# Three probability tiles of a Perceiver kernel turned by DMA instead of TensorE, and weight loads moved behind the experts

## The reference, cut to what matters

```python
# first cross attention (16 heads of 64), keys beyond a length masked out
scores = einsum('bhmk,bhnk->bhmn', Q, K);  scores = where(mask == 0, -1e20, scores)
attn = softmax(scores / 8);  ctx = einsum('bhmn,bhnv->bhmv', attn, V);  x = x + ctx @ W_o
# small self attention on the 64 tokens, then a mixture of 8 experts
x = x + self_attention(layernorm(x)) ; x = x + experts(layernorm(x))
# second cross attention over the same context, then the delta-rule mixer (weights d_w, w1s)
# last feed-forward part: weights quantised to 8 bit, which needs the largest |w| of each channel
amax = clip(max(abs(w)), 1e-8);  scale = 127 / amax;  w_q = clip(round(w * scale), -128, 127) / scale
```

## Time and profile before

| | us |
|---|---|
| median of 3 runs | 409.58 |
| lowest, highest | 409.54, 411.42 |
| profiled execution, its own time | 409.08 |
| its span | 407.3 |
| TensorE busy | 382.6 (94%) |
| TensorE weight loads, beside it | 296.9 (73%) |
| VectorE busy | 287.2 (71%) |
| ScalarE busy | 287.6 (71%) |
| GpSimd busy | 237.9 (58%) |

### The profile page before, as it was taken

One profiled execution on the slowest core, in us unless ns is written; L12 is line 12 of the kernel. 1 busy time (PEld: TensorE's weight loads), 2 busy tenths in 40 slices (PEclk: granted clock), 3 DMA queues, 4 the chain that ended last, 5 costly groups with the idle time before them and its releaser, 6 DMA issues.

```text
span 407.3 us, 11598 instructions
## 1 busy us (share of the span) xinstructions
PE 382.6 (94%) x4632; PEld 296.9 (73%) x4632; DVE 287.2 (71%) x730; ACT 287.6 (71%) x568; POOL 237.9 (58%) x196
## 2 busy tenths in 40 slices
PE   6988999999998999988989999999999999999995
PEld 3446777777776778967966777777777769878874
DVE  2788888888875777566767767877787777454544
ACT  3477888888787887746429988899888987544240
POOL 2497989999974659301006997877788668030000
PEclk9899999999999999998999999999999999999999
DMA  8899998989999998990005999999999999600000
GB/s 305 323 253 167 201 182 134 178 147 212 228 184 210 223 178 132 338 408 21 3 2 84 185 200 207 195 196 191 194 193 191 189 199 188 276 2 3 2 2 3
DMA packets 188390, 68.56 MB, mean 168 GB/s; under 512 B 183200, under 2 KB 183984, under 8 KB 187440
## 3 DMA queue, kind: packets, MB, share of 16 engines
q1 hardware_dynamic: 188048, 66.77, 82.2%
q10 hardware_dynamic: 288, 1.05, 0.8%
HBM read 21.90 MB, written 0.03 MB: 54 GB/s over the span
## 4 chain that ended last, share of the span: by engine, by line
PE 46%; DVE 17%; DMA 10%; POOL 10%; ACT 9%; issue 7%; SPq 0%; POOLq 0%; DVEq 0%; ACTq 0%
PE ps L521 17%; PE ps L489 13%; DMA probsT<-halves 9%; DVE probs L640 8%; POOL halves L593 7%; ACT probs L558 3%; PE ps L501 2%; ACT halves L565 2%; PE ps L1097 2%; DMA moe<-in_ctxT 2%; PE ps L764 1%; DVE U L653 1%; PE ps L1204 1%; DVE halves L593 1%; PE ps L774 1%
## 5 line engine op out<-in xcount | busy, mean ns | idle before, releaser
L593 POOL TENSOR_TENSOR halves<-probs,halves 128x896 f16<-128x896 f32 x75 | 141.7, 1892 | 55.2 <-ACT halves L565 53.7
L521 PE MATMUL ps<-ctxN,probsT 128*128 128x128 f16 x2352 | 148.4, 219 | 4.2 <-DMA probsT<-halves 4.1
L521 PEld LDWEIGHTS ps<-ctxN,probsT 128*128 128x128 f16 x2352 | 139.4, 98 | 17.8 <-issue 7.0
L489 PE MATMUL ps<-ctxT_parts,GT_parts 128*128 128x512 f16 (+1 forms) x660 | 143.0, 353 | 5.6 <-DVE negmax L640 5.4
L558 ACT ACTIVATE probs<-probs,shifted 128x896 f32<-128x896 f32 x112 | 115.5, 1031 | 6.7 <-DVE shifted L645 6.7
L489 PEld LDWEIGHTS ps<-ctxT_parts,GT_parts 128*128 128x128 f16 x660 | 59.6, 98 | 54.9 <-DVE negmax L640 7.6
L565 ACT CAST halves<-probs 128x896 f16<-128x896 f32 x93 | 85.8, 923 | 0.0
L653 DVE SCALAR_TENSOR_TENSOR U<-U,alpha,ps 128x128 f32<-128x128 f32 x112 | 38.6, 345 | 55.2 <-PE ps L521 54.9
L640 DVE CUSTOM_DVE_ANT_0 probs<-ps,zero,negmax 128x896 f32<-128x896 f32 x56 | 67.5, 1205 | 1.7 <-POOL halves L593 1.2
L640 DVE CUSTOM_DVE_ANT_0 probs<-ps,maskb,negmax 128x896 f32<-128x896 f32 x56 | 67.5, 1205 | 1.6 <-issue 0.7
L555 ACT ACTIVATE alpha<-negmax 128x1 f32<-128x1 f32 x96 | 28.2, 294 | 37.8 <-DVE negmax L640 36.6
(11 more groups left out here) (368 smaller groups left out, 388.7 us busy)
## 6 DMA issues: line engine op xcount, KB each, us to landing
moe<-in_ctxT SPq DMA_DIRECT2D x7, 448.0 KB, 7.6
moe<-in_mask SPq DMA_DIRECT2D x6, 448.0 KB, 10.1
moe<-in_gateT SPq DMA_DIRECT2D x2, 1024.0 KB, 9.3
moe<-in_upT SPq DMA_DIRECT2D x2, 1024.0 KB, 11.0
moe<-in_downT SPq DMA_DIRECT2D x2, 1024.0 KB, 13.7
moe<-in_fir_long SPq DMA_DIRECT2D x1, 2048.0 KB, 9.7
probsT<-halves SPq DMA_TRANSPOSE x93, 4.8
wv<-in_wv SPq DMA_DIRECT2D x2, 512.0 KB, 7.1
```

What stands on the lines that cost most here:

```text
L489: ins = pe.matmul(ps[:, 2 * b + h, 0:width], GT_parts[:, g_part, r * P:(r + 1) * P], ctxT_parts[:, keys:keys + width], start=(g_part == 0 ...
L521: ins = pe.matmul(ps[:, bank, 0:D], probsT_parts[:, b, p_part, k * P:(k + 1) * P], ctxN_parts[:, at:at + D], start=(p_part == 0 and c_part ...
L593: eng.tensor_tensor(halves_of(L, n)[:, 1, :], probs[:, n % BUFS, :], halves_of(L, n)[:, 0, :], ALU.subtract).then_inc(lower_of(L, n)[0], 1)
```

## The change

Tiles 15, 31 and 47 of the first attention are no longer turned on TensorE: they go by DMA, and VectorE does their halving. `win`, `wout`, `d_w` and `w1s` are no longer loaded between the transpositions of the first attention but behind the expert loads, ahead of the wait for `y_ready`; `a_w` moves from tile 40 to tile 36. The channel maxima of `win` and `wout` move on VectorE from before `y_ready` to behind the probabilities of the small self attention.

```diff
         WEIGHTS_AT = {24: ("in1", w_qT, "wqT1"), 27: ("in1", wkT[:], "wkT1"), 30: ("out0", wv[:], "wv0"),
-                      33: ("out0", wo[:], "wo0"), 36: ("ffn", win[:], "win"), 38: ("ffn", wout[:], "wout"),
-                      40: ("small_attn", a_w[:], "a_w"), 42: ("delta", d_w[:], "d_w"), 44: ("delta", w1s[:], "w1s")}
+                      33: ("out0", wo[:], "wo0"), 36: ("small_attn", a_w[:], "a_w")}
 
         def on_pe(L, n):
-            return L == 0 and n % 4 == 3 and n > 4 or n >= STEPS - 3 or n == STEPS - 5
+            return L == 0 and n % 4 == 3 and n % 16 != 15 and n > 4 or n >= STEPS - 3 or n == STEPS - 5
 
         def on_vector(L, n):
             if L == 0:
-                return n in (0, 2) or 4 <= n < 30 and n % 4 == 1
+                return n in (0, 2) or 4 <= n < 30 and n % 4 == 1 or n % 16 == 15
             return n >= RAMP and n % 4 == 3
@@ SP's queue
             load_experts(0)
             load_experts(1)
+            load("ffn", win[:], "win")
+            load("ffn", wout[:], "wout")
+            load("delta", d_w[:], "d_w")
+            load("delta", w1s[:], "w1s")
             sp.wait_ge(sem("y_ready"), 1)
@@ VectorE, behind project_dve(dve, 0)
-            loaded(dve, "ffn")
-            for i, w in enumerate((win, wout)):
-                ins = dve.tensor_reduce(wamx[:, i * FT:(i + 1) * FT], w[:], AX, ALU.max, apply_absolute_value=True)
-            seq(ins)
             loaded(dve, "par")
@@ VectorE, behind the second half of a_probs
+            loaded(dve, "ffn")
+            for i, w in enumerate((win, wout)):
+                ins = dve.tensor_reduce(wamx[:, i * FT:(i + 1) * FT], w[:], AX, ALU.max, apply_absolute_value=True)
+            seq(ins)
             seq(dve.tensor_scalar(wamx[:], wamx[:], 1e-8, None, ALU.max))
```

## The result

The changed kernel took 410.74 us (median of 20 runs, 408.81 to 413.52) beside 409.56 us for the kernel before on the same chip (median of 20 runs); the ratio is 1.0031, 95% interval [1.0016, 1.0046]. That is inside the predicted range and inside the 0.5% that were called no change, but it is a small loss and not nothing. The sum of the forecast came close; several of its parts did not.

A forecast was written before the change was run, and what follows sets the result against it. The prediction took the loop as tight in several places, TensorE having 46% of the chain of waits. Its terms, 0 + 0 - 0.4 + 0 + 0.65 = +0.25 us, gave 409.6 us, range 407.6 to 411.6.

The forecast's parts named there:

- Tile 15, 0: First attention: GpSimd's gapless work holds the maximum of tile 20 at 70.77, so no gain; bounds -0.76 and +0.5 us.
- Rival 3: Tile 15: GpSimd's mask conversion blocks VectorE's new halving, about +1 us, 410.6; chance 0.06.
- Tile 31, 0: First attention: halving waits up to 0.9 us for GpSimd, later given back; 0, bounds -0.76 and plus one transposition, 2.4 us.
- that is given back in front of GpSimd's halving of tile 33: Tile 31: the halving's delay of up to 0.9 us vanishes where tile 37's maximum waits for GpSimd anyway.
- rival 2: Tile 31: the DMA queue takes over, one transposition of 2.4 us added to tile 34's landing, total +2.65, 412.0; chance 0.11.
- Tile 47, -0.4: End of first attention: VectorE's halving fits a gap before tile 43's addition; gain 0.4 us, bounds -0.76 and 0.
- it carries to the end: Tile 47: the 0.4 us gain passes through GpSimd's chain and the last transposition to the end of the first attention.
- Loads, 0: Moving weight loads out of the first attention gains 0, since TensorE waits for no landing from 125 to 161 us.
- Maxima, +0.65: Behind the small self attention's probabilities: the two reductions, 1.28 us, make the copy of `oT` 0.65 us late, nothing absorbing it.
- Rival 4: The maxima run under cover because the `oT` copy is late for another reason: -0.4 us, 409.1; chance 0.11.
- Rival 1: TensorE bounds the whole first attention and all three turns come off: -1.65 us, 407.8; chance 0.18.
- Rival 5: `win` and `wout` land late and VectorE waits, each microsecond over 3 us of delay counting in full; chance 0.02.

The follow-up runs named there:

- e7: The kernel before with tile 31 alone turned by DMA and halved by VectorE; ratio to before 1.0009 [0.9987, 1.0031].
- e1: The kernel before with tiles 15, 31 and 47 by DMA, loads and maxima at their old places; ratio to before 1.0045 [1.0018, 1.0071].
- e4: The changed kernel with `wo` loaded after tile 38 instead of 33; ratio to before 0.9997 [0.9974, 1.0020].
- e6: The changed kernel with the warm-up between the attentions replaced by one of about 44 more TensorE instructions; ratio to before 1.0054 [1.0032, 1.0077].
- e8: The kernel before with tile 47 alone turned by DMA and halved by VectorE; ratio to before 1.0012 [0.9992, 1.0031].
- e2: The changed kernel with tiles turned as before, so only loads and maxima are moved; ratio to before 1.0003 [0.9981, 1.0025].
- e5: The kernel before with 44 fewer TensorE warm-up instructions between the attentions, 12 instead of 56; ratio to before 1.0015 [0.9996, 1.0035].
- e9: The kernel before with tile 15 alone turned by DMA and halved by VectorE; ratio to before 1.0006 [0.9986, 1.0026].
- e12: The changed kernel with turns as before, `wo` behind tile 38, maxima in VectorE's gaps among the experts; ratio to before 0.9970 [0.9947, 0.9994].
- e10: The kernel before with the load of `wo` moved from behind tile 33 to behind tile 39; ratio to before 0.9994 [0.9977, 1.0010].
- e11: The kernel before with `wo` loaded behind tile 32 instead of 33 and `win` behind 33 instead of 36; ratio to before 0.9975 [0.9954, 0.9997].

## Why the prediction was right in sum and wrong in its parts

- **Tile 15, 0.** Right, with its reason: the maximum of tile 20 at the same place, and the halving not stopped by the mask conversion (1.09 us inside it). Rival 3 is out.
- **Tile 31, 0.** The step that failed is "that is given back in front of GpSimd's halving of tile 33". It is given back in part only: alone the tile costs 0.7 us in the trace (e7). I had reasoned that GpSimd's run does not hang on the turn and let the delay end there. But the 0.94 us that the halving costs at tile 29 are more than the 0.78 of the turn, and behind that run lies tile 34's landing, with no slack in the queue: it comes at 103.2 us or later from the first maximum with tile 31 on the queue and at 103.0 or earlier without. In e1, e4 and e6 TensorE waited for tile 31 itself as well, 0.85, 1.02 and 0.21 us. The price in e7 is less than a third of rival 2's 2.4 us, and the place is rival 2's.
- **Tile 47, -0.4.** The step that failed is "it carries to the end". The first half of it held: VectorE's wait for TensorE shrank by 1.0 us, and from tile 43 on the values products come 0.77 us earlier relative to tile 34, all of the turn and not only the 0.4 that I took. But 0.3 of it are gone at tile 50, and 0.74 at tile 52, because its transposition took 5.86 us from the queue instead of 5.11. So the last values products come 0.26 us later relative to tile 34, where the prediction named 0.3 to 0.8 earlier as its sign. I had bounded this tile by -0.76 and 0. Over six executions with it on the queue it came out from -0.79 (e6, nearly all of the turn kept to the end) to +0.94 (e8, with a wait for its own landing). One more transposition on the queue had been priced for tile 31 and not for tile 47, and the instruction packets were in no term at all.
- **Loads, 0.** Not quite: the first attention is 0.6 us shorter with them gone (e2), against my argument that TensorE does not wait for a landing from 125 to 161 us. Of that, 0.3 is there at tile 34, where e5, e8 and e9 have it as well with the loads in place, so it is the difference of executions. The other 0.3 comes at tile 52, behind the stretch that I had looked at: its transposition took 4.87 us in e2 and 4.84 in e12, and 5.11 to 5.33 in before, e5, e9, e10 and e11, where loads stand in the queue after tiles 40 to 44.
- **Maxima, +0.65.** Right: +0.56 in the trace, 0.5 over the middle parts of all kernels. Rival 4 is out.
- **Sum.** In terms of the first attention, +0.7 + 0.65 - 0.6 = +0.75 from the single kernels, against +0.47 in the trace of after; with the maxima's 0.5 that is +1.0 to 1.25. The median is 1.2 us higher. The agreement is worth little, since each term comes from one execution and that of tile 47 alone varies by more than 1 us. That the forecast of +0.25 came within 1 us of it is in part luck: tile 31 was put at 0 and, by most executions, tile 47 at -0.4 too low, the loads at 0 too high, and of the terms that were not 0 only the maxima's +0.65 is borne out in size. The rest of the trace's differences, +0.4 in the second attention, -0.3 at the start and the clock, is of the size in which executions and instruction counts vary, and I do not assign it.
- **The sign.** The prediction called itself wrong if a second wait for a landing appeared in the first attention. There were two before already, 1.87 and 0.15 us; what appeared is that the second grew to 0.89.
- **The rivals.** Rival 1 is out: the turns did not come off. Rival 2 was the right place and got 0.11, since it was priced at 2.4 us for a whole transposition; it came at 0.7 for tile 31, and with the fall of the clock (e1) at 2.8 for the three. Rival 5 is out: VectorE does not wait for `win`, the first reduction starts at 187.87 without idle time.

## What to carry to other kernels

Work that leaves a busy engine for a queue must be priced at the queue's next late landing and not only at the engine it leaves. Look for where the queue is idle (54 GB/s ahead of tile 33's transposition here, 326 with the load put there): a load belongs there. Moving the one load `wo` shortened the first attention by 1.5 us in the trace of e10; three turns less for TensorE lengthened it. And before the difference of two traces is laid to a change, set aside the stretches in which the granted clock differs, and compare loops whose code is the same in both.

## What the runs showed of the hardware that I had not expected

- The granted clock fell to 0.50 (1.2 GHz) for about 3.4 us (once for about 7) in 10 of the 14 profiled executions, at 12, 125, 187 to 190 or 388 to 390 us. It cost 1.7 us at 125, 0.4 to 0.5 at 190, and 1.4 to 1.8 at 390 (rest 56.67 and 57.09 instead of 55.3). Runs of the kernel before with no fall still lie between 407.1 and 410.6 us, so executions of one kernel differ by more than this change is worth, with the clock and without.
- A packet of 16 KB of TensorE's instructions makes the transposition under way later. In the second attention, in all 14 traces, those that meet no packet of instructions land 4.0 to 5.0 us after their issue; of each pair that meets one of TensorE's, the later is mostly at 5.7 to 6.9 us.
- 44 instructions of warm-up more or fewer changed which transpositions of an untouched loop are late (e5, e6), and whether a packet met tile 47's transposition went with 4.4 to 4.7 or 6.2 to 6.4 us for it.
